# The cross-attention's weights and the gate's weights transposed by VectorE in 32x32 blocks by way of DRAM, in place of TensorE

## The chip, the core and the metric

The kernel runs on one core of a Trainium2 chip. The metric is the time of one execution on the device, in microseconds (us), as the median of several runs. The core's engines run side by side, each through its own fixed list of instructions: TensorE (PE in the rows; PEld is its loading of weights), VectorE (DVE), ScalarE (ACT), GpSimd (POOL) and SyncE (SP), which here only issues DMA transfers. They meet at semaphores. TensorE reads SBUF and writes PSUM.

## What is computed

`x` holds 64 sequences of 128 tokens of 128 channels in float32, and `ctx` 64 contexts of 77 tokens. Two stages follow each other, both with a residual:

```python
x = x + tanh(g_xattn[0]) * cross_attention(ctx, layernorm(x), Wk, Wq, Wv)
x = x + tanh(g_ffn[0])   * moe_attention(layernorm(x), sim, gates, q, k, v, o)

# moe_attention, per token, 16 experts
logits = xn @ sn - sigmoid(gates)              # xn, sn of unit length
w = softmax of relu(logits) over active experts (top 2 where none is active)
q, k, v = sum over e of w[n, e] * (x[n] @ proj[e])     # three projections
o = softmax(q k^T / sqrt(128)) v
out = sum over e of w[n, e] * (o[n] @ o_proj[e])
```

The weights of the cross-attention's softmax (128 queries by 77 keys for a sequence) are needed with the keys on the partitions, and the gate's weights `w` (tokens on the partitions, 16 experts by 4 sequences on the free axis) are needed as rows, a row of 512 tokens for an expert. Both are transposes.

## The kernel before, in words

The 64 sequences are worked in 16 groups of four (`G = 4`, 512 tokens, one PSUM bank of 512 columns). The program is written out in full by a Python loop: a head, then passes `i` of 16 steps `s`, one step for each expert. Every engine has its own `body(i)`, in which the order is written by hand: what stands at step `s` runs after the step's expert work.

In pass `i`, TensorE runs the 9 products of expert `s` for group `i` (`experts`, L1176: three projections, each as high and low halves in float16: `zq` high with `w_hi`, `zq` high with `w_lo`, `zq` low with `w_hi`), and every second step a pair of chunks of the output projection of group `i-1` or `i-2` (`y_pair`, L1188, six products). Among these lie the small products of the other groups: in pass `i` the cross-attention of group `g1 = i + 2`, and the second layer norm and the gate of group `g2 = i + 1`, and the expert attention of `gc = i - 1`.

The operand of the experts is made in a chain of three engines: VectorE multiplies `x2T_p` by a broadcast row of the gate's weights into `zq_full` (`zq_scale`, L957, four steps ahead of TensorE, `LEAD = 4`), ScalarE rounds it to the high half (`zq_high`, L612), GpSimd subtracts to get the low half (`zq_low`, L538).

The gate's path of group `g2`: the logits' products on TensorE lie among the experts of step 4 (L1231). VectorE reads them (`gate_logits` at step 4, L903 to L909), makes the mask (`gate_mask`, step 5) and the weights `w_new` (`gate_softmax`, step 6, L946). TensorE transposes `w_new` at step 8 (`w_transpose`, L1282), ScalarE copies it from PSUM to `wT` (`wT_out`, L681), SyncE writes it to the DRAM tensor `w_rows` (L405), and reads it back, two experts at a time, spread over all partitions (`spread`, `wq_bc<-w_rows`, L412, 512 KB in SBUF each, eight a group).

The cross-attention's path of group `g1`: scores at step 9 (L1239), VectorE's maximum (`x_max`, L1013), ScalarE's exponentials at step 10 (`x_exps`, L688, four), TensorE's transposes at step 12 (`px_transpose`, L1296, four of 128x77), ScalarE's copy to `pxT` (`pxT_out`, L706), and at step 14 the product with the values (`att_product`, L1303). Then VectorE adds it to `x_all` (L1024) and takes the statistics of the second layer norm.

Also at step 12 ScalarE runs `y_scale(gc, 2)` behind `pxT_out`: 8 scaled copies of the third pair's banks (L625), which TensorE's fourth pair at step 14 waits for, as it writes the same banks. At step 7 TensorE makes the output of the expert attention (`oT_p<-pcT,v_sb`, L1379), ScalarE rounds it (L791), VectorE takes the low half (`oT_low`, L972), and the first pair at step 8 waits for that.

Three other transposes already go another way: VectorE transposes 32x32 blocks (`blocks_transposed`, L892), SyncE writes the blocks to the DRAM tensor `blk_rows` (L394) and reads them back in an order in which each partition gets its row (L400, four DMAs), and a copy by ScalarE puts them in place (for instance `xn_mix` to `xnT`, L661). They serve `xn`, the expert attention's weights `pc` and its values `v`.

## Time and profile before

| | us |
|---|---|
| median of 3 runs | 841.78 |
| lowest, highest | 841.29, 841.80 |
| the profiled execution, its own time | 841.99 |
| its span, from the first to the last instruction | 839.9 |
| busy: TensorE / VectorE / GpSimd / ScalarE | 796.5 / 583.7 / 481.0 / 434.2 |
| mean granted clock of TensorE | 0.997 of full speed |

2.1 us of the profiled execution lie outside its span. All durations below come from this one execution. TensorE's products overlap in its pipeline: a product of 512 columns is shown with 0.38 us, but the next one starts 0.216 us later; what a product costs is read from the starts of its neighbours. In a timeline a row is one instruction or several of a kind in a row, with the first start and the whole length; in square brackets stands the idle time ahead and who ended it. The chain of waits goes back from the last instruction to what released each one. DMA issues stand under SPq.

### The profile page before, as it was taken

The numbers are of one execution on the slowest core, as the hardware profiler recorded it, in microseconds if no ns is written. First come the engines' busy times: TensorE is split into PE (matmuls) and PEld (weight loads), VectorE is DVE, ScalarE is ACT, GpSimd is POOL, SyncE is SP. The second block draws the span as 40 slices with busy tenths as digits, with TensorE's granted clock in tenths as the row PEclk, the third lists the DMA queues.
The fourth block names the chain that finished last, engine by engine and source line by source line (L and its number), as shares of the span: only waits on it lengthen the run. The fifth ranks groups of instructions, "written<-read, shape, count | busy, mean of one in ns | idle before, by whom it ended". The sixth has DMA issues, their size and how long they took to land.

```text
span 839.9 us, 13842 instructions
## 1 busy us (share of the span) xinstructions
PE 796.5 (95%) x4111; PEld 431.5 (51%) x4111; DVE 583.7 (69%) x1993; ACT 434.2 (52%) x1134; POOL 481.0 (57%) x702
## 2 busy tenths in 40 slices
PE   5579999999999999999999999999999999999995
PEld 4345555555555555555555555555555555544442
DVE  3767676768587676758767675876767586676647
ACT  4555646455454645545464554546455454543433
POOL 3265656564665656466665646666564665655524
PEclk9999999999999999999999999999999999999998
DMA  6373453534444333444333434443244443325100
GB/s 188 98 240 120 153 183 115 154 132 131 140 145 128 112 117 131 122 140 151 126 121 95 143 121 140 151 124 129 72 149 131 140 150 117 113 59 184 65 9 25
DMA packets 71099, 106.40 MB, mean 127 GB/s; under 512 B 6960, under 2 KB 45552, under 8 KB 71024
## 3 DMA queue, kind: packets, MB, share of 16 engines
q1 hardware_dynamic: 70304, 105.44, 40.1%
q8 instruction: 32, 0.52, 0.2%
q14 instruction: 43, 0.35, 0.1%
q10 hardware_dynamic: 720, 0.08, 0.1%
HBM read 89.51 MB, written 15.99 MB: 126 GB/s over the span
## 4 chain that ended last, share of the span: by engine, by line
PE 74%; DVE 14%; DMA 4%; issue 3%; ACT 3%; POOL 1%; SPq 1%; DVEq 0%; ACTq 0%; POOLq 0%
PE acc_q L1176 16%; PE acc_k L1176 16%; PE acc_v L1176 16%; PE y L1188 7%; PE oT_p L1188 7%; DVE x_all L986 4%; DVE zq_full L957 2%; PE oT_p L1379 2%; DVE logit L906 2%; PE m L1248 2%; PE m L1303 1%; PE m L1289 1%; ACT y_sc L625 1%; PE m L1239 1%; DMA stage<-in_L_ffn_k_proj_dram 1%
## 5 line engine op out<-in xcount | busy, mean ns | idle before, releaser
L538 POOL TENSOR_TENSOR zq<-zq_full,zq 128x512 f16<-128x512 f32 x256 | 294.9, 1161 | 298.7 <-ACT zq L612 297.5
L612 ACT ACTIVATE zq<-zq_full 128x512 f16<-128x512 f32 x256 | 160.8, 640 | 246.2 <-DVE zq_full L957 243.7
L1176 PE MATMUL acc_q<-zq,w_hi 128*128 128x512 f16 x512 | 194.6, 380 | 2.8 <-POOL zq L538 2.8
L1176 PE MATMUL acc_k<-zq,w_hi 128*128 128x512 f16 x512 | 194.5, 380 | 0.0
L1176 PE MATMUL acc_v<-zq,w_hi 128*128 128x512 f16 x512 | 194.5, 380 | 0.0
L986 DVE SCALAR_TENSOR_TENSOR x_all<-y,w_out,x_all 128x128 f32<-128x128 f32 x356 | 121.8, 342 | 80.1 <-issue 71.2
L957 DVE TENSOR_TENSOR zq_full<-wq_bc,x2T_p 128x512 f32<-128x512 f32 x256 | 167.4, 672 | 3.3 <-DMA wq_bc<-w_rows 2.5
L986 DVE SCALAR_TENSOR_TENSOR x_all<-oT_p,w_out,x_all 128x128 f32<-128x128 f32 x356 | 121.3, 341 | 0.0
L552 POOL TENSOR_TENSOR x_all<-y_sc,x_all 128x128 f32<-128x128 f32 x240 | 100.3, 454 | 20.1 <-DVE x_all L986 13.3
L1176 PE MATMUL acc_q<-zq,w_lo 128*128 128x512 f16 x256 | 97.3, 380 | 0.0
L1176 PE MATMUL acc_v<-zq,w_lo 128*128 128x512 f16 x256 | 97.3, 380 | 0.0
L1176 PE MATMUL acc_k<-zq,w_lo 128*128 128x512 f16 x256 | 97.2, 380 | 0.0
L1188 PE MATMUL y<-w_hi,oT 128*128 128x512 f16 x236 | 89.4, 379 | 4.1 <-issue 4.1
L1188 PE MATMUL oT_p<-w_hi,oT 128*128 128x512 f16 x236 | 89.4, 379 | 0.0
L1176 PEld LDWEIGHTS acc_v<-zq,w_hi 128*128 128x128 f16 x512 | 53.9, 105 | 53.9 <-issue 0.6
L1176 PEld LDWEIGHTS acc_q<-zq,w_hi 128*128 128x128 f16 x512 | 52.1, 102 | 54.0 <-issue 3.4
L1024 DVE SCALAR_TENSOR_TENSOR x_all<-m,rsum_x,x_all 128x128 f32<-128x128 f32 x64 | 18.0, 344 | 87.2 <-PE m L1303 87.2
L1176 PEld LDWEIGHTS acc_k<-zq,w_hi 128*128 128x128 f16 x512 | 50.1, 98 | 53.9 <-issue 0.6
L1188 PE MATMUL oT_p<-w_lo,oT 128*128 128x512 f16 x118 | 44.7, 379 | 0.0
L1188 PE MATMUL y<-w_lo,oT 128*128 128x512 f16 x118 | 44.6, 378 | 0.0
L625 ACT ACTIVATE y_sc<-oT_p,w_out 128x128 f32<-128x128 f32 x116 | 33.0, 369 | 19.9 <-PE oT_p L1188 19.9
L1176 PEld LDWEIGHTS acc_k<-zq,w_lo 128*128 128x128 f16 x256 | 27.0, 105 | 26.9 <-issue 0.3
(191 smaller groups left out, 1110.0 us busy)
## 6 DMA issues: line engine op xcount, KB each, us to landing
wq_bc<-w_rows SPq DMA_DIRECT2D x128, 512.0 KB, 4.4
out_dram<-x_all SPq DMA_DIRECT2D x16, 256.0 KB, 6.8
blk_rows<-v_blk SPq DMA_DIRECT2D x15, 256.0 KB, 4.2
v_mix<-blk_rows SPq DMA_DIRECT2D x60, 64.0 KB, 2.0
blk_rows<-pc_blk SPq DMA_DIRECT2D x15, 256.0 KB, 3.3
pcT<-blk_rows SPq DMA_DIRECT2D x60, 64.0 KB, 2.0
blk_rows<-xn_blk SPq DMA_DIRECT2D x13, 256.0 KB, 2.6
xn_mix<-blk_rows SPq DMA_DIRECT2D x52, 64.0 KB, 3.4
```

Of the source, the lines that this page charges most:

```text
L538: nc.gpsimd.tensor_tensor(zq[:, 1, e % Z_SLOTS, :], zq_full[:, e % F_SLOTS, :], zq[:, 0, e % Z_SLOTS, :], ALU.subtract).then_inc(zq_lo_poo ...
L552: nc.gpsimd.tensor_tensor(total, y_sc[:, n % 2, b, j, :], total, ALU.add).then_inc(y_pool_added, 1)
L612: nc.scalar.activation(zq[:, 0, e % Z_SLOTS, :], zq_full[:, e % F_SLOTS, :], ACT.Copy).then_inc(zq_hi_done, 1)
L625: last = nc.scalar.activation(y_sc[:, n % 2, b, j, :], bank[:, tok(j)], ACT.Copy, scale=w_out[:, g % 2, e, b0 + b:b0 + b + 1])
L906: link(nc.vector.tensor_tensor(logit[:], logit[:], sig[:].unsqueeze(1).broadcast_to([P, G, E]), ALU.subtract), 1)
L957: nc.vector.tensor_tensor(zq_full[:, e % F_SLOTS, :], wq_bc[:, e // 2 % W_SLOTS, e % 2], x2T_p[:], ALU.mult).then_inc(zq_full_done, 1)
L986: nc.vector.scalar_tensor_tensor(out=rows(x_all, g, b0 + b), in0=bank[:, tok(j)], scalar=w_out[:, g % 2, e, b0 + b:b0 + b + 1], in1=rows(x ...
L1024: last = nc.vector.scalar_tensor_tensor(out=rows(x_all, g, b), in0=m1[:, tok(b)], scalar=rsum_x[:, b:b + 1], in1=rows(x_all, g, b), op0=AL ...
L1176: last = nc.tensor.matmul(acc[m][:], w[:, m, s, :], zq[:, half, s % Z_SLOTS, :], start=(s == 0 and n == 0), stop=(s == E - 1 and n == 2))
L1188: last = nc.tensor.matmul(bank[:], oT[:, g % 2, half, tok(b)], w[:, O, QUAD * k:QUAD * (k + 1), :].rearrange("p e c -> p (e c)"), start=(n ...
L1248: done = nc.tensor.matmul(m1[:, tok(b)], qT[:, tok(b)], kT[:, tok(b)], start=True, stop=True)
L1379: last = nc.tensor.matmul(oT_p[:, tok(b)], v_sb[:, b, :], pcT[:, :, b, :], start=True, stop=True)
```

## The change

`w_transpose` and `wT_out` are gone. Behind `w_new` VectorE now transposes it in 32x32 blocks to `w_blk` (one instruction, 128x64, at step 6), and SyncE writes it to `w_rows` with four DMAs in place of one. `w_new` loses its zero half.

`px_transpose` stays for groups 0 and 1 alone (`P_HEAD = 2`). For the other 14 groups VectorE transposes `px` in blocks at step 11 (one instruction, 128x384; `px` is padded from 77 to 96 keys, zeroed once by GpSimd in place of `w_new`), SyncE writes `px_blk` to the DRAM tensor `px_rows`, waits for it, and reads it back with three DMAs (32, 32 and 13 keys) at step 12, and `pxT_out` copies from `px_mix` in SBUF.

```diff
+P_HEAD = 2
+S_PAD = 96
@@ SyncE
             def weight_rows(g):
-                wait(sp, wT_sb, g + 1)
-                sp.dma_start(w_rows[bass.ds(g, 1)].rearrange("a r n -> (a r) n"), wT[:]).then_inc(w_rows_in, 16)
-                wait(sp, w_rows_in, 16 * g + 16)
+                wait(sp, w_blk_done, g + 1)
+                for i in range(4):
+                    sp.dma_start(w_rows[g, :, 32 * i:32 * (i + 1)].rearrange("(k c) t -> c k t", k=2),
+                                 w_blk[32 * i:32 * (i + 1)]).then_inc(w_rows_in, 16)
+                wait(sp, w_rows_in, 64 * (g + 1))
...
+                    if s == 12 and has(g1):
+                        n = g1 - P_HEAD
+                        wait(sp, px_blk_done, n + 1)
+                        wait(sp, px_mix_in, 48 * n)
+                        sp.dma_start(px_rows.rearrange("i t r -> (i t) r"),
+                                     px_blk[:].rearrange("p j b n -> p (j b n)")).then_inc(px_blk_out, 16)
+                        wait(sp, px_blk_out, 16 * (n + 1))
+                        wait(sp, pxT_sb, g1)
+                        for j in range(3):
+                            keys = min(32, S - 32 * j)
+                            sp.dma_start(px_mix[32 * j:32 * j + keys].rearrange("t i b n -> t i (b n)"),
+                                         px_rows[:, 0:keys, P * j:P * (j + 1)].rearrange("i t r -> t i r")
+                                         ).then_inc(px_mix_in, 16)
@@ GpSimd
-            nc.gpsimd.memset(w_new[:], 0.0)
+            nc.gpsimd.memset(px[:], 0.0).then_inc(pool_set, 1)
@@ ScalarE
-            def wT_out(g):
-                wait(act, wT_ps, g + 1)
-                wait(act, w_rows_in, 16 * g)
-                nc.scalar.activation(wT[:], m0[0:E * G, 0:P], ACT.Copy).then_inc(wT_sb, 1)
...
             def pxT_out(g):
-                wait(act, pxT_ps, g + 1)
                 wait(act, att_ps, g)
-                nc.scalar.activation(pxT[:], m1[0:S, :], ACT.Copy).then_inc(pxT_sb, 1)
+                if g < P_HEAD:
+                    wait(act, pxT_ps, g + 1)
+                    nc.scalar.activation(pxT[:], m1[0:S, :], ACT.Copy).then_inc(pxT_sb, 1)
+                else:
+                    wait(act, px_mix_in, 48 * (g - P_HEAD + 1))
+                    nc.scalar.activation(pxT[:].rearrange("p (b i n) -> p b i n", b=G, n=32),
+                                         px_mix[:].rearrange("p i b n -> p b i n"), ACT.Copy).then_inc(pxT_sb, 1)
@@ VectorE, end of gate_softmax (step 6)
+                wait(dve, w_ready, g + 1)
+                wait(dve, w_rows_in, 64 * g)
+                nc.vector.transpose(w_blk[:], w_new[:, g % G_SLOTS].rearrange("p (k c) b -> p k (c b)", k=2)
+                                    ).then_inc(w_blk_done, 1)
@@ VectorE, body
+                    if s == 11 and has(g1):
+                        wait(dve, xexp_done, g1 + 1)
+                        wait(dve, px_blk_out, 16 * (g1 - P_HEAD))
+                        blocks_transposed(px_blk, px[:], px_blk_done)
@@ TensorE
-                    if s == 8 and has(g2):
-                        w_transpose(g2)
-                    if s == 12 and has(g1):
-                        px_transpose(g1)
```

How the instructions stand now is shown at three places of a pass in the middle of the program. First SyncE from step 7 to step 0 of the next pass, before:

```order
L391 DMA ctx_g<-in_ctx_dram 77x4x128 [waits ctxT_ps]
L405 DMA w_rows<-wT 64x128 [waits wT_sb]
L412 DMA wq_bc<-w_rows 128x1024 [waits zq_full_done,w_rows_in]
L412 DMA wq_bc<-w_rows 128x1024 [waits zq_full_done] x2
L422 DMA out_dram<-x_all 128x4x128 [waits y_pool_added,y_added]
L412 DMA wq_bc<-w_rows 128x1024 [waits zq_full_done] x4
```

The same stretch of SyncE now:

```order
L398 DMA ctx_g<-in_ctx_dram 77x4x128 [waits ctxT_ps]
L414 DMA w_rows<-w_blk 32x2x32 [waits w_blk_done]
L414 DMA w_rows<-w_blk 32x2x32 x3
L422 DMA wq_bc<-w_rows 128x1024 [waits zq_full_done,w_rows_in]
L422 DMA wq_bc<-w_rows 128x1024 [waits zq_full_done] x2
L432 DMA out_dram<-x_all 128x4x128 [waits y_pool_added,y_added]
L422 DMA wq_bc<-w_rows 128x1024 [waits zq_full_done]
L495 DMA px_rows<-px_blk 128x384 [waits px_mix_in,px_blk_done]
L501 DMA px_mix<-px_rows 32x4x128 [waits pxT_sb,px_blk_out]
L501 DMA px_mix<-px_rows 32x4x128
L501 DMA px_mix<-px_rows 13x4x128
L422 DMA wq_bc<-w_rows 128x1024 [waits zq_full_done] x3
```

The write of the gate's weights became four, and the four DMAs of `px` came in between the fourth and the fifth spread of the gate's weights.

Second, VectorE at steps 6 to 8, before, from the gate's last steps to the low half of `oT`:

```order
L944 RECIPROCAL wsum<-wsum 128x4 [waits gate_step]
L946 TENSOR_TENSOR w_new<-mask,wsum 128x4x16 [waits w_out_done,gate_step]
L957 TENSOR_TENSOR zq_full<-wq_bc,x2T_p 128x512 [waits zq_lo_pool]
L963 TENSOR_SCALAR rs_d<-rsum_c,out_scale 128x4 [waits rsum_c_done,scales_done]
L967 TENSOR_TENSOR w_out<-w_new,rs_d 128x64 [waits y_scaled,y_added,w_out_done]
```

VectorE at the same place now:

```order
L967 RECIPROCAL wsum<-wsum 128x4 [waits gate_step]
L969 TENSOR_TENSOR w_new<-mask,wsum 128x4x16 [waits w_out_done,gate_step]
L974 STREAM_TRANSPOSE w_blk<-w_new 128x64 [waits w_rows_in,w_ready]
L984 TENSOR_TENSOR zq_full<-wq_bc,x2T_p 128x512 [waits zq_lo_pool]
L990 TENSOR_SCALAR rs_d<-rsum_c,out_scale 128x4 [waits rsum_c_done,scales_done]
L994 TENSOR_TENSOR w_out<-w_new,rs_d 128x64 [waits y_scaled,y_added,w_out_done]
```

One transpose came in behind `w_new`, ahead of the `zq_full` of step 7. (The transpose of `px` stands likewise at step 11, between a `zq_full` and the additions of the second pair.)

Third, ScalarE from step 10 to step 14 now:

```order
L709 ACTIVATE px,sum_x<-m,nmax_x 128x77 [waits rsum_x_done,px_blk_done,xmax_done]
L709 ACTIVATE px,sum_x<-m,nmax_x 128x77 x3
L717 ACTIVATE vx<-m 77x512 [waits att_ps,vx_ps]
L635 ACTIVATE zq<-zq_full 128x512 [waits zq_used,zq_full_done]
L722 ACTIVATE x2T_p<-x2T 128x512 [waits zq_full_done,x2T_sb]
L731 ACTIVATE pxT<-px_mix 77x512 [waits px_mix_in,att_ps]
L648 ACTIVATE y_sc<-oT_p,w_out 128x128 [waits y_pool_added,y_ps,w_out_done]
```

The order is that of before, but the copy to `pxT` waits for the last of three DMAs where it waited for TensorE, and `y_scale` stands behind it.

## Rows read from the trace of the kernel before

**Rows 1.** The page, part 1: busy time and share of each engine

```profile
PE 796.5 (95%) x4111; PEld 431.5 (51%) x4111; DVE 583.7 (69%) x1993; ACT 434.2 (52%) x1134; POOL 481.0 (57%) x702
```

**Rows 2.** Chain of waits, pass 7, steps 8 and 12: start, length, what

```profile
406.30 0.11 PE m L1282
406.41 0.37 issue
406.78 0.81 PE y L1188 x3
...
418.89 0.44 PE m L1296 x4
```

**Rows 3.** Chain of waits over the whole span: TensorE's `scores`, once a pass

```profile
287.54 0.89 PE m L1248 x8
...
335.72 0.89 PE m L1248 x8
...
384.77 0.89 PE m L1248 x8
```

**Rows 4.** Timeline of TensorE, pass 7, step 14: start, length, instruction

```profile
424.34 1.06 PE L1303 MATMUL m<-vx,pxT 77*128 77x128 f32 x8
425.23 0.38 PE L1188 MATMUL y<-w_hi,oT 128*128 128x512 f16 x1
```

**Rows 5.** Timelines of VectorE and GpSimd, pass 7, steps 3 to 8

```profile
391.59 0.68 DVE L892 STREAM_TRANSPOSE pc_blk<-pc 128x512 f32<-128x512 f32 x1
...
393.91 1.19 DVE L906 TENSOR_TENSOR logit<-logit,sig 128x64 f32<-128x64 f32 x1
...
401.71 0.27 DVE L946 TENSOR_TENSOR w_new<-mask,wsum 128x64 f32<-128x64 f32 x1
...
405.99 0.69 DVE L972 TENSOR_TENSOR oT<-oT_p,oT 128x512 f16<-128x512 f32 x1 [2.13 <-ACT oT L791]
...
393.86 1.16 POOL L538 TENSOR_TENSOR zq<-zq_full,zq 128x512 f16<-128x512 f32 x1 [1.68 <-ACT zq L612]
```

**Rows 6.** Timelines of ScalarE and VectorE, pass 7, steps 10 to 12

```profile
413.46 0.21 ACT L688 ACTIVATION_READ_ACCUMULATOR px<-m,nmax_x 128x1 f32 x1
...
419.36 0.59 ACT L706 ACTIVATE pxT<-m 77x512 f32<-77x512 f32 x1 [0.79 <-PE m L1296]
420.98 1.14 ACT L625 ACTIVATE y_sc<-oT_p,w_out 128x128 f32<-128x128 f32 x4 [1.03 <-PE oT_p L1188]
...
415.10 0.35 DVE L986 SCALAR_TENSOR_TENSOR x_all<-y,w_out,x_all 128x128 f32<-128x128 f32 x1 [1.54 <-issue]
```

**Rows 7.** Timelines of VectorE and GpSimd, pass 5, step 4

```profile
296.68 0.22 DVE L906 TENSOR_TENSOR logit<-logit,sig 128x64 f32<-128x64 f32 x1
...
296.99 1.16 POOL L538 TENSOR_TENSOR zq<-zq_full,zq 128x512 f16<-128x512 f32 x1 [2.03 <-ACT zq L612]
```

**Rows 8.** Round trip of `pc`, pass 1: issue, end (PE); page part 6: landing

```profile
103.15 0.43 SPq L394 DMA_DIRECT2D blk_rows<-pc_blk  x1
...
110.33 1.13 PE oT_p L1379 x8
...
xn_mix<-blk_rows SPq DMA_DIRECT2D x52, 64.0 KB, 3.4
```

**Rows 9.** Writes of the gate's weights: issue in pass 7; landing of all 16

```profile
406.75 0.45 SPq L405 DMA_DIRECT2D w_rows<-wT  x1
...
DMA to landing us min/median/max: 1.7/2.2/3.8
```

**Rows 10.** Timelines of ScalarE and TensorE, pass 0, steps 10 and 14

```profile
79.13 0.21 ACT L688 ACTIVATION_READ_ACCUMULATOR px<-m,nmax_x 128x1 f32 x1
...
87.42 1.06 PE L1303 MATMUL m<-vx,pxT 77*128 77x128 f32 x8
```

**Rows 11.** Head: timeline of VectorE, then the chain of waits

```profile
36.21 0.27 DVE L946 TENSOR_TENSOR w_new<-mask,wsum 128x64 f32<-128x64 f32 x1
...
38.95 3.27 DMA w_rows<-wT
```

More of the change, by code:

```diff
@@ L966, in out_weights @@
                 wait(dve, y_scaled, 4 * (g - 1))
[L967 removed]
+                nc.vector.tensor_tensor(w_out[:, g % 2], w_new[:, g % G_SLOTS],
                                         rs_d[:].unsqueeze(1).broadcast_to([P, E, G]), ALU.mult).then_inc(w_out_done, 1)
@@ L1276, in kx_product @@
                 nc.tensor.matmul(m1[:, 0:G * S], m_kq[:], ctxT[:], start=True, stop=True).then_inc(kxT_ps, 1)
-            def w_transpose(g):
-                wait(pe, w_ready, g + 1)
-                if g == X_HEAD - 2:
-                    wait(pe, xnT_sb, X_HEAD)
-                nc.tensor.transpose(m0[:, 0:P], w_new[:, g % G_SLOTS].rearrange("p h e b -> p (h e b)"),
-                                    ident[:]).then_inc(wT_ps, 1)
             def vx_product(g):
-                wait(pe, wT_sb, cap(g))
+                wait(pe, logit_read, cap(g))
                 wait(pe, xnT_sb, g + 1)
@@ L1295, in px_transpose @@
                 for b in range(G):
-                    last = nc.tensor.transpose(m1[0:S, tok(b)], px[:, b, :], ident[:])
+                    last = nc.tensor.transpose(m1[0:S, tok(b)], px[:, b, 0:S], ident[:])
                 last.then_inc(pxT_ps, 1)
```

31 lines of the change are left out of this document (17 added, 14 removed).

## The prediction, made before the changed kernel ran

> **What bounds the kernel now.** The first view is the page's busy table: TensorE is busy for 95% of the span, the next engine for 69% [rows 1]. So what the change takes from TensorE counts, if nothing else is late where it is taken. Whether it is shows in the second view, the chain of waits. Over the whole span it passes TensorE's `scores` once a pass: from pass to pass 49.05 us (335.72 to 384.77), and 48.18 us in one pass (287.54 to 335.72) [rows 3]. The distance is the same from pass 2 to pass 13 but for that one, so pass 7, around 400 us, stands for them. In it the chain leaves TensorE once: between the logits of step 4 and the first output pair of step 8 it runs over VectorE (L906, the additions, the mask, a `zq_full`) and ScalarE, and TensorE waits for what comes out. From step 8 to the next step 4 it stays on TensorE. That split decides the two halves of the change, since one of the removed transposes lies in each part.
>
> **Gate transpose on TensorE: worth nothing in most passes.** The transpose takes 0.11 us of TensorE at 406.30, and behind it TensorE stands still for 0.37 us until the output pair starts at 406.78 [rows 2]. That start is set by VectorE: the low half of `oT` starts at 405.99, takes 0.69 us, ends at 406.68 [rows 5], and the pair follows 0.1 us later. Nothing in the chain to that instruction passes through the removed transpose or ScalarE's copy of it, which stands behind ScalarE's work on `oT`. So without it TensorE waits 0.48 us in place of 0.37, and the pair starts when it did. Gain 0. Only in pass 1, where the pair is not yet waiting for VectorE, is 0.11 us gained.
>
> **Transposes of the cross-attention's weights: 0.44 us each.** At step 12 four of them take 0.44 us, in the stretch in which the chain never leaves TensorE [rows 2]. 14 of 16 groups lose them, in passes 0 to 13. Full worth would be 14 x 0.44 = 6.2 us. It is full worth only where the new way round is ready for step 14.
>
> **The new way round, in a pass of the middle.** The last exponential ends at 413.67 (413.46 + 0.21) [rows 6]. VectorE is idle then, for 1.54 us until 415.10, where it waits for the second output pair [rows 6], so its new transpose costs its neighbours nothing. The same instruction on 512 columns takes 0.68 us [rows 5]; for 384 I take 0.56, and it ends at 414.28. Then come a DMA out, a wait, three DMAs in. The nearest row is the round trip of `pc` in pass 1, the one place where TensorE waited for such a trip: issued at 103.15, with TensorE released at 110.33, that is 7.2 us with four DMAs in and 256 KB [rows 8]. Here they are three and 192 KB: less one issue of 0.43 us, and a little for the size, 6.6 us. The data are in at 420.9, and ScalarE's copy (0.65 us with its start, as the copy from PSUM now takes 0.59 [rows 6]) ends at 421.6. Who waits? First the product of step 14, which stood at 424.34 [rows 4] and would like to start 0.44 us earlier, at 423.9: 2.3 us to spare. Second, and tighter, the 8 scaled copies queued behind it on ScalarE: the first four take 1.14 us from 420.98 [rows 6], all eight about 2.2, and the fourth output pair, at 425.23 [rows 4] and then 424.79, waits for them. Counting back, with 0.07 us for the release, the copy to `pxT` may end at 422.5; it ends at 421.6. So 0.9 us to spare, and the trip may take up to 7.5 us before a pass loses anything, 8.0 until the gain is gone.
>
> **What else moves.** VectorE's transpose of `w_new` (128x64, 0.25 us with its wait, as its neighbours of that size, `w_new` itself 0.27 [rows 5]) lies ahead of an idle time of 2.13 us that ends with L972 [rows 5], so it is hidden; if that cover were gone it would cost 0.25 us a pass. SyncE issued the write of the weights at 406.75 [rows 9]; `w_new` is done at 401.98 [rows 5], so the four writes can go from 402.3 on, 0.45 us apart as the one of now, and even with the slowest landing of such a write in the trace (3.8 us, against 2.2 in the median [rows 9]) the spreads start earlier than now. That also clears the queue ahead of the trip of `px`. Behind SyncE's new wait at step 12 stand the fifth and sixth spreads, which VectorE needs six steps later: nothing. The scaled copies start at 421.6 in place of 420.98, so GpSimd gets its two `zq` of steps 13 and 14 about 0.6 us later and may hand the second norm on some 0.5 us late; I cost it at nothing, as ScalarE and TensorE have other work ahead of what needs it, and at 0.5 us a pass if they hadn't. ScalarE's own 16 copies of the gate's weights are gone, off the chain.
>
> **Pass 0** has no output pairs, so its steps are shorter. The exponentials end at 79.34 and the product of step 14 starts at 87.42 [rows 10], to become 86.9 without the two transposes. The new way: 79.34 + 0.6 for VectorE + 6.6 to 7.2 for the trip + 0.65 for the copy = 87.2 to 87.8. I take 87.6: 0.2 us later than now. Bounds: 0.55 us gained if the trip is hidden, 1.5 lost if it takes 1.3 us more.
>
> **The head.** `w_new` of group 0 is done at 36.48, but the write to DRAM is issued only at 38.95, behind TensorE and ScalarE, and lands 3.27 us later [rows 11], so the first spread goes at 42.2. Now the first of four writes goes at 36.8 and the last at 38.2. If it lands in 2.2 to 3.8 us [rows 9] the spread starts at 40.4 to 42.0, 0.2 to 1.8 us earlier. I take 1.1.
>
> Here the Trainium skill speaks against the change. The row shows one write landing in 3.27 us [rows 11]. The page "DMA: Bandwidth & Descriptors", Specifications, says that pieces under 512 bytes are below line rate, as the engine then reads, modifies and writes; the four writes of the gate's weights go in pieces of 128 bytes, which no row here has on this path. By that rule they land late, and the head's gain would fall to its lower end, with the sum 0.9 us higher. In the passes it would change nothing, as there are over 2 us to spare.
>
> **The sum.** Passes 2 to 13: 12 x 0.44 = 5.3 us gained. Pass 1: 0.44 + 0.11 = 0.55. Pass 0: 0.2 lost. Head: 1.1. Together 6.7 us. Against the profiled execution's 841.99 us that is 835.3, and as that lies 0.2 above the median of 841.78, the median becomes 835.1. By the bounds of pass 0 and the head alone: 833.5 to 837.5. I add 1 us above for small waits that I don't see: 833 to 838.5.
>
> **Rivals.** First, **a turn-over between VectorE and GpSimd**. L906, an operation of 0.22 us, takes 1.19 us at 393.91, and ends when GpSimd's L538, started at 393.86, 0.05 us before it, ends [rows 5]. In pass 5 L906 came first (296.68 against 296.99), took 0.22 us [rows 7], and that pass is the one of 48.18 us: 0.87 us shorter [rows 3]. So two instructions race with a margin of 0.05 us, and the winner is worth 0.87 us a pass. If the change shifts GpSimd's or ScalarE's queue by more than that up to step 4, 12 further passes gain: 12 x 0.87 = 10.4 us, and 824.7. For it: ScalarE and GpSimd are shifted by some 0.5 us at steps 13 to 0. Against it: both have idle time ahead of the race (GpSimd waits 1.68 us for ScalarE [rows 5]), and both racers start from the same output pair of step 2. 18%. The page "SBUF — State Buffer", Who interferes with whom, has the rule: an operation with two inputs in SBUF and one of GpSimd that reads SBUF exclude each other, and issue order decides; by that rule, the trace agrees with 1.19 against 0.22 us.
>
> Second, **slower: the round trip of `px` comes late.** Place: ScalarE's copy to `pxT` at step 12 with the scaled copies behind it. It decides from 8.0 us on, and costs 1 us a pass for each us beyond. For it: the trips in the loop share the queue with 512 KB spreads, and the reads back of `xn` land in 3.4 us in the median [rows 8]: with that, and the last of three issues 0.86 us behind the first, a way out of 3.7 us already gives 8.0, just the point. With 8.6 us, 13 passes lose 0.6 each: 13 x 0.6 = 7.8, less 1.1 of the head, so 848.5 (841.78 + 6.7). Against it: the spreads are earlier now. 14%.
>
> Third, **no gain**: trip and queue take 7.5 to 8.0 us, or GpSimd's lateness reaches TensorE's transposes of step 2, and the 0.44 us are waited away in each pass. Then the head's gain is what stays: 841.78 - 1.1 = 840.7, within 838.5 to 842. 16%.
>
> **How the numbers follow.** Forecast 52%: 835.1, in its own range 833 to 838.5. Turn-over 18%: 824.7. No gain 16%. Slower 14%: from 843.5 on. The range takes in forecast, turn-over and most of the third case, and leaves out the slower one and a little: 824.5 to 841. About 0.2% (1.7 us) is what a measurement of this kernel can tell from no change: faster means under 840.1. Forecast, turn-over and half the third give 0.78; same 0.10; slower 0.12.
>
> **What would show it.** In the trace after: the distance of `scores` from pass to pass falls from 49.05 to 48.6; the wait of the first output pair behind step 8's experts grows to about 0.5 us; TensorE has no wait at step 14; ScalarE's copy to `pxT` ends 3 us ahead of it, with the trip of `px` at 6.6 us; L906 stays at 1.19 us; the first spread is issued at about 41; TensorE is busy for less by the transposes. Wrong would be: a distance near 47.7 with L906 at 0.22 (the first rival); idle time of TensorE at step 14 ahead of an output pair, released by ScalarE's `y_sc` (the second); a distance of 49 with new waits at step 2 (the third).

## The result, and the profile after

Before and after, six runs each: 841.65 us (840.91 to 842.15) against **833.17 us** (831.46 to 837.11); ratio 0.9907, 95% interval 0.9881 to 0.9932. The change makes the kernel about 8.5 us faster. The forecast was 835.1 us in a range of 824.5 to 841.0. Note the spread: 1.2 us for the kernel before, 5.6 us for the changed one. The execution profiled is the slowest of the six, 837.11 us with a span of 835.3, and 4.9 us under the profiled one of before (841.99). So its rows have to explain both why it is faster and why others are faster still.

The page of the changed kernel, part 1: busy time of each engine.

```profile
PE 790.2 (95%) x4039; PEld 423.4 (51%) x4039; DVE 593.7 (71%) x2023; ACT 430.0 (51%) x1118; POOL 481.2 (58%) x702
```

TensorE has 72 instructions and 6.3 us less than in [rows 1], VectorE 30 and 10 us more.

The chain of waits at the `scores` of passes 5 to 8, and the first output pair of step 8 of pass 2 from the timeline of TensorE (start, length, instruction, idle ahead of it):

```profile
288.78 0.89 PE m L1279 x8
...
337.67 0.89 PE m L1279 x8
...
386.30 0.89 PE m L1279 x8
...
434.21 0.89 PE m L1279 x8
```

```profile
164.91 0.38 PE L1219 MATMUL y<-w_hi,oT 128*128 128x512 f16 x1 [0.48 <-issue]
```

The distance from pass to pass, 49.05 us in [rows 3], is 48.63 us in most passes (pass 7, 386.30 to 434.21, and three others, explained below, have 47.7 to 47.9; pass 5, 288.78 to 337.67, has 48.89). The wait ahead of the pair is 0.48 us, 0.11 more than in [rows 2]. From the `scores` of pass 2 (142.88) to those of pass 14 (768.98) the kernel gains 7.1 us. But pass 2 itself starts 2.5 us **later** than before (142.88 against 140.39). So the passes gained more than forecast, and the beginning, where 1.45 us were to be won, lost.

Two rows show the first half of that loss. Timeline of TensorE in pass 0, step 2, and its windows (us, busy and instructions, granted clock, DMA share, GB/s), changed kernel:

```profile
56.88 1.11 PE L1286 MATMUL m<-ident,x 128*128 128x128 f32 x4 [2.99 <-ACT x L656]
```

```profile
56.00:60.00 4.00, 3.12 (x10) 0.50 0.64 193
60.00:64.00 4.00, 4.00 (x18) 0.66 0.64 198
```

The experts' products of pass 0 start 2.5 us earlier than before, but the second norm that pass 0 needs next is only 1.4 us earlier, so TensorE stands still for 2.99 us (1.04 before). Behind that the granted clock is 0.50, the lower of its two levels (1.2 GHz), and products of 512 columns come 0.43 us apart, where they come 0.216 us apart at 1.00.

The clock of the first products needs care. The profile's record of the granted clock begins only at 40 to 55 us (49.1 in this execution, 53.2 in the one before), and ahead of its first entry a window prints 1.00 whatever the clock was; the mean of 0.997 given for the kernel before leaves that stretch out too. The spacing of the products fills the gap. In all 14 traces of this document the first products of pass 0 come 0.43 us apart. Two neighbours in the kernel before:

```profile
50.55 0.63 PE L1176 MATMUL acc_k<-zq,w_hi 128*128 128x512 f16 x1
50.98 0.63 PE L1176 MATMUL acc_k<-zq,w_lo 128*128 128x512 f16 x1
```

How long that lasts differs from execution to execution: to 48.9 us in this one, to 53.1 in the one before, to 50.6 in the run with the gate's half alone (1, below). That early change here is the rest of the 2.99 us: with the same head, but a clock that rose later, TensorE stood still for 1.80 us there.

The second half of the loss is the new trip in pass 0, here from SyncE, ScalarE and TensorE (write out, reads back, copy, product of step 14):

```profile
80.70 0.32 SPq L495 DMA_DIRECT2D px_rows<-px_blk  x1
85.89 1.25 SPq L501 DMA_DIRECT2D px_mix<-px_rows  x3
88.64 0.63 ACT L731 ACTIVATE pxT<-px_mix 77x512 f32<-77x512 f32 x1 [4.41 <-DMA px_mix<-px_rows]
...
89.32 0.94 PE L1327 MATMUL m<-vx,pxT 77*128 77x128 f32 x6 [1.46 <-ACT pxT L731]
```

"Trip" means, from here on, from the issue of that write (80.70) to the start of ScalarE's copy (88.64): 7.94 us here and 8.74 us in pass 1, where the fourth output pair waits 0.88 us for `y_sc`. In pass 2 it is 6.47 us, and nobody waits:

```profile
172.44 0.98 SPq L495 DMA_DIRECT2D px_rows<-px_blk  x1
176.17 1.24 SPq L501 DMA_DIRECT2D px_mix<-px_rows  x3
178.91 0.63 ACT L731 ACTIVATE pxT<-px_mix 77x512 f32<-77x512 f32 x1 [2.20 <-DMA px_mix<-px_rows]
...
182.03 1.06 PE L1327 MATMUL m<-vx,pxT 77*128 77x128 f32 x8
```

Two more numbers for later: `px_blk` takes 0.578 us each and `w_blk` 0.245 us; the four small writes of the gate's weights land in 1.3/1.5/3.9 us (minimum, median, maximum), the single write of before in 1.7/2.2/3.8 [rows 9].

**Where the extra gain in the passes comes from.** VectorE's subtraction of the sigmoid (L929, L906 before) against GpSimd's `zq` (L561), in a usual pass of the changed kernel (3) and in pass 7:

```profile
200.60 1.16 POOL L561 TENSOR_TENSOR zq<-zq_full,zq 128x512 f16<-128x512 f32 x1 [1.68 <-ACT zq L635]
200.65 1.19 DVE L929 TENSOR_TENSOR logit<-logit,sig 128x64 f32<-128x64 f32 x1
```

```profile
395.43 0.22 DVE L929 TENSOR_TENSOR logit<-logit,sig 128x64 f32<-128x64 f32 x1
395.88 1.16 POOL L561 TENSOR_TENSOR zq<-zq_full,zq 128x512 f16<-128x512 f32 x1 [1.56 <-ACT zq L635]
```

This is the race of [rows 5] and [rows 7]. "Turned over" means that VectorE comes first and its subtraction is short. Among passes 2 to 13 of the profiled execution of before that was so in one pass; in this one in four (subtractions at 395.43, 589.25, 636.99 and 684.86). Three more passes at 0.72 to 0.9 us each, less 0.26 us lost in pass 5, are what the passes gained beyond 12 x 0.42.

### The profile page after: what moved, and what is told of

Its sections match the earlier page's. It is cut to its first block, busy times and chain, and to the rows that moved or that the text cites. A ratio compares the mean times of both kernels' runs of the same rounds, so it can differ in the third digit from the quotient of the medians.

```text
span 835.3 us, 13855 instructions
## 1 busy us (share of the span) xinstructions
PE 790.2 (95%) x4039; PEld 423.4 (51%) x4039; DVE 593.7 (71%) x2023; ACT 430.0 (51%) x1118; POOL 481.2 (58%) x702
## 4 chain that ended last, share of the span: by engine, by line
PE 73%; DVE 12%; DMA 5%; ACT 4%; issue 3%; SPq 2%; POOL 1%; DVEq 0%; ACTq 0%; POOLq 0%
PE acc_q L1207 16%; PE acc_k L1207 16%; PE acc_v L1207 15%; PE y L1219 8%; PE oT_p L1219 7%; DVE x_all L1013 4%; DVE zq_full L984 2%; DMA px_rows<-px_blk 2%; PE oT_p L1402 2%; ACT y_sc L648 2%; PE m L1279 2%; PE m L1327 2%; DVE logit L929 1%; PE m L1270 1%; PE m L1313 1%
## 5 line engine op out<-in xcount | busy, mean ns | idle before, releaser
L561 POOL TENSOR_TENSOR zq<-zq_full,zq 128x512 f16<-128x512 f32 x256 | 295.9, 1165 | 294.0 <-ACT zq L635 293.8
L1219 PEld LDWEIGHTS y<-w_hi,oT 128*128 128x128 f16 x236 | 22.9, 97 | 31.2 <-ACT oT L816 7.6
```

The costliest lines, as they stand in the source:

```text
L561: nc.gpsimd.tensor_tensor(zq[:, 1, e % Z_SLOTS, :], zq_full[:, e % F_SLOTS, :], zq[:, 0, e % Z_SLOTS, :], ALU.subtract).then_inc(zq_lo_poo ...
L1219: last = nc.tensor.matmul(bank[:], oT[:, g % 2, half, tok(b)], w[:, O, QUAD * k:QUAD * (k + 1), :].rearrange("p e c -> p (e c)"), start=(n ...
```

## Experiments

Theory going in: the passes gain by the cross-attention's transposes alone (0.44 us each); the gate's is worth nothing there; the beginning loses by the fallen clock and by two long trips; the race is a separate cost of 0.87 us a pass. Rivals: the gate's transpose counts too; the fall of the clock is not tied to the idle time; the subtraction is long for another reason. "Scores of pass 2" is the start of TensorE's `scores` there in the timeline: 140.23 before, 142.72 in the changed kernel.

### 1 and 2: one half of the change alone

Gate alone (cross-attention's weights transposed by TensorE in every pass; SyncE's and VectorE's steps for them run only from `P_HEAD` on, and so never):

```diff
-P_HEAD = 2
+P_HEAD = 99
+                    if s == 12 and has(g1):
+                        px_transpose(g1)
```

Cross-attention alone (gate part as before):

```diff
-                nc.vector.transpose(w_blk[:], ...).then_inc(w_blk_done, 1)
+                    if s == 8 and has(g2):
+                        w_transpose(g2)
...
-                for i in range(4):
-                    sp.dma_start(w_rows[g, :, 32 * i:32 * (i + 1)]...)
+                sp.dma_start(w_rows[bass.ds(g, 1)].rearrange("a r n -> (a r) n"), wT[:]).then_inc(w_rows_in, 16)
```

> Only the gate's weights are transposed by VectorE by way of DRAM; the cross-attention's weights stay with TensorE in every pass. Theory (the gate transpose is worth nothing in a pass, since TensorE then waits for VectorE before the first output pair of step 8; it brings only an earlier first expert product): distances of the scores stay 49.05 us, that wait is 0.48 instead of 0.37 us, and the time is 839 to 842 against 841.7, the upper end if the early start is given back to a fallen clock in pass 0. Rival (its removal counts in every pass, 0.11 x 12): another 1.3 us less and distances of 48.94.

> Only the cross-attention's weights go over VectorE and DRAM; the gate's stay with TensorE and ScalarE. Theory: all of the gain in the passes comes from here: distances of 48.6 us, so 12 x 0.44 = 5.3 us less than before from pass 2 on, less up to 1.5 us lost in passes 0 and 1 by the long trips there: 836 to 837.5. No 2.99 us idle of TensorE and no fallen clock at 56 to 62 us. If the gate part were worth something in a pass, this would be worse than the changed kernel by more than 1 us.

**Gate alone: 840.2 us** (839.46 to 841.18, 11 runs), ratio 0.9983 (0.9974 to 0.9992). Every distance from pass 2 to pass 13 is 49.05 to 49.07 us, the wait ahead of the pair at step 8 is 0.48 us:

```profile
209.36 0.38 PE L1219 MATMUL y<-w_hi,oT 128*128 128x512 f16 x1 [0.48 <-issue]
```

So in this surrounding the gate's transpose is worth nothing in a pass, as the theory has it. What it gains, 1.6 us, it gains at the beginning: scores of pass 2 at 138.11, 2.1 us earlier than before. Its head is that of the changed kernel, but the wait ahead of the second norm is 1.80 us and not 2.99, and no fall of the clock follows at 56 to 62 us. (Its record shows 0.50 at 44 to 51 us. That is the slow stretch of the first products; the other records, but for kernel 4's, begin too late to show it.)

**Cross-attention alone: 833.2 us** (831.54 to 835.37, 4 runs), ratio 0.989 (0.9876 to 0.9904): as fast as the whole change, and faster than expected (836 to 837.5). No clock fell at 56 to 62 us; the first products were slow until 54.5. What the traced execution shows of the difference is again the race, turned over in four of the twelve passes from 2 to 13. At 835.37 us it is the slowest of the four executions; that the faster ones have more such passes was seen in no trace.

### 3: TensorE kept busy in pass 0

```diff
+                    if s == 2 and i == 0:
+                        for r in range(12):
+                            nc.tensor.matmul(y0[:], w_hi[:, K, 2, :],
+                                             w_hi[:, Q, 0:4, :].rearrange("p e c -> p (e c)"), start=True, stop=True)
                     if s == 2 and has(g2):
                         x2_transpose(g2)
```

> The changed kernel, with 12 products (2.6 us) that nobody reads put into TensorE's idle 2.99 us ahead of the second-norm transposes of pass 0. Theory (the granted clock fell to 0.50 at 56 to 62 us because TensorE had been idle there, at a cost of about 2.3 us): the clock stays near 1.00 there, the products are 0.216 us apart, and the time is 2 to 2.5 us less than the changed kernel's in executions in which its clock falls. Rival (the fall has another cause, or comes in one execution and not in another): clock still 0.50 there, or a time equal to the changed kernel's fastest (831.5).

The same windows of TensorE in this kernel:

```profile
56.00:60.00 4.00, 4.00 (x22) 1.00 0.68 178
60.00:64.00 4.00, 4.00 (x26) 1.00 0.72 215
```

The clock stays up, `scores` of pass 1 start at 93.94 instead of 96.15: 2.2 us, the expected amount. But this doesn't show that the 12 products did it. In this execution the first products were slow until 52.2 us and not only until 48.9, so TensorE came to this place at 55.3, and the second norm's data were ready at 56.8, as in the changed kernel: without the 12 products it would have waited some 1.5 us, not 2.99. What speaks for the idle time as the cause is the comparison of traces. Of the eleven without such products, two have a fall at 56 us, and they are the two with the longest wait at this place (2.99 us, and 2.88 in kernel 8); the other nine have at most 1.86 us and no fall there. Kernels 7 and 8 wait once more in pass 0, for 2.92 and 2.48 us, and there too a fall follows.

And yet the **time is 835.31 us** (832.25 to 836.47, 6 runs), no better than the changed kernel's 833.17. The expectation of the time failed. The profiled execution (835.47 us) shows one reason: of the twelve passes from 2 to 13 only two were turned over. The 2.2 us at the beginning are of the size of two and a half turned-over passes, and the number of those differs from execution to execution; so does the clock of the first products. As long as the race runs, a time of this kernel can't answer a question of 2 us. So the race had to go first.

### 4 and 5: the race taken away, in both kernels

An operand in PSUM instead of SBUF for the subtraction (4 is the changed kernel with it, 5 the kernel before with it):

```diff
-                nc.vector.tensor_tensor(logit[:], lg, rnorm2[:]...broadcast_to([P, G, E]), ALU.mult)
+                lg2 = m0[:, G * E:2 * G * E].rearrange("p (b e) -> p b e", e=E)
+                nc.vector.tensor_tensor(lg2, lg, rnorm2[:]...broadcast_to([P, G, E]), ALU.mult)
...
-                nc.vector.tensor_tensor(logit[:], logit[:], sig[:]..., ALU.subtract)
+                nc.vector.tensor_tensor(logit[:], lg2, sig[:]..., ALU.subtract)
```

> The changed kernel, in which the scaled gate logits are kept in PSUM between the two steps, so that the subtraction of the sigmoid reads one operand from SBUF and one from PSUM. Theory (the 1.19 us subtraction of 0.22 us stands behind GpSimd's subtraction because both of its operands are in SBUF; it is worth 0.87 us a pass): the subtraction takes about 0.2 us in all passes, distances of 47.75 instead of 48.6 in the 8 passes that had it long, so 7 to 8 us less: 824 to 826. Rival (one SBUF operand is enough to be held up, or TensorE then waits for something else next): 1.19 us and no change, or a gain of less than 3 us.

> The kernel before, with only the scaled gate logits kept in PSUM, as in the run that took the changed kernel to 825.5. Theory (the collision with GpSimd is a cost of its own, 0.87 us a pass, that does not depend on who transposes): the subtraction is short in every pass, distances of 48.18 instead of 49.05 in the passes 2 to 12 that had it long, so 10 to 11 us less than before: 831 to 832. The change would then be worth 5 to 6.5 us between the two kernels without the collision. Rival (the change frees the queue of VectorE so that the collision matters only with it): less than 5 us less than before.

**4: 825.53 us** (824.8 to 827.94, 5 runs), ratio 0.9814 (0.9801 to 0.9826), and **5: 830.84 us** (830.63 to 831.35, 4 runs), ratio 0.9872 (0.9858 to 0.9887). Both as the theory expected. VectorE and GpSimd in the changed kernel with the edit:

```profile
194.66 1.16 POOL L562 TENSOR_TENSOR zq<-zq_full,zq 128x512 f16<-128x512 f32 x1 [1.68 <-ACT zq L636]
194.72 0.22 DVE L936 TENSOR_TENSOR logit<-m,sig 128x64 f32<-128x64 f32 x1
```

The order is the losing one, GpSimd first by 0.06 us, and the subtraction takes 0.22 us all the same: it is short in all 16 groups of both kernels. So it was held up only while both of its operands lay in SBUF. The distances are 47.77 us (changed) and 48.22 (before): the difference of 0.45 us is the four transposes, and 10.6 us of the kernel before (841.46 us, measured beside 5) had been this one wait. Without the race the change is worth 830.84 - 825.53 = 5.3 us.

### 6: the halves again, without the race

The kernel with cross-attention alone, and the edit of 4:

> The cross-attention's weights by VectorE and DRAM, the gate's weights by TensorE and ScalarE, logits kept in PSUM. It differs from the 825.5 us kernel in the gate's transpose alone. Theory (the gate's transpose hid in TensorE's wait for VectorE at step 8; without the collision that wait is gone, so the transpose now counts): distances of 47.88 instead of 47.77, which is 1.3 us over 12 passes, and with the later start of the head 827.5 to 829. Rival (the gate part is worth nothing anywhere): 825.5 within 0.7.

**6: 831.19 us** (830.13 to 832.63, 4 runs), ratio 0.9872 (0.9854 to 0.989). That is 5.7 us more than the whole change, where 2 to 3.5 were expected, and as much as the kernel before with the same edit: here the cross-attention's half alone is worth **nothing**. Its trips are 7.9 to 8.5 us long, those of the 825.5 us kernel 6.5 to 7.9, six of eleven under 7.0 (passes 2 to 12). SyncE's timeline in a pass of each, cross-attention alone first:

```profile
210.39 0.49 SPq L415 DMA_DIRECT2D w_rows<-wT  x1
212.21 1.29 SPq L422 DMA_DIRECT2D wq_bc<-w_rows  x3
213.66 0.39 SPq L432 DMA_DIRECT2D out_dram<-x_all  x1
216.89 0.32 SPq L422 DMA_DIRECT2D wq_bc<-w_rows  x1
217.62 0.32 SPq L495 DMA_DIRECT2D px_rows<-px_blk  x1
222.79 1.24 SPq L501 DMA_DIRECT2D px_mix<-px_rows  x3
```

```profile
202.26 1.71 SPq L415 DMA_DIRECT2D w_rows<-w_blk  x4
205.03 2.55 SPq L423 DMA_DIRECT2D wq_bc<-w_rows  x3
210.32 0.39 SPq L433 DMA_DIRECT2D out_dram<-x_all  x1
213.54 0.32 SPq L423 DMA_DIRECT2D wq_bc<-w_rows  x1
214.27 0.32 SPq L496 DMA_DIRECT2D px_rows<-px_blk  x1
218.08 1.24 SPq L502 DMA_DIRECT2D px_mix<-px_rows  x3
```

The write of the blocks goes out 28.87 us after the pass's `scores` in both (188.75 and 185.41). But the three spreads of 512 KB start 5.4 us ahead of it in the first and 9.2 us in the second. Windows just ahead of that write and over it (us, granted clock, DMA share, GB/s), first kernel, then second:

```profile
216.00:217.00 1.00, 1.00 1.06 254
217.00:218.00 1.00, 1.00 0.95 372
218.00:219.00 1.00, 1.00 1.09 369
```

```profile
212.00:213.00 1.00, 1.00 0.18 51
213.00:214.00 1.00, 1.00 0.00 0
214.00:215.00 1.00, 1.00 0.43 152
```

In the first the write enters DMA engines that are full, in the second empty ones. The expectation had the wrong mechanism (the 0.11 us of TensorE). The new theory: the gate's half is worth most of the 5.7 us because its earlier writes clear the DMA engines ahead of the other half's trip.

### 7, 8 and 9: the trip made longer, its traffic moved

A second write in the trip (7); the gate's writes and spreads held back (8), both in the 825.5 us kernel; and the store of the output (`out_dram<-x_all`) moved behind the trip in the 831.2 us kernel (9):

```diff
+                        sp.dma_start(px_more.rearrange("i t r -> (i t) r"),
+                                     px_blk[:].rearrange("p j b n -> p (j b n)")).then_inc(px_more_out, 16)
+                        wait(sp, px_more_out, 16 * (n + 1))
                         wait(sp, pxT_sb, g1)
                         for j in range(3):
```

```diff
                     if s == 9 and has(g2):
+                        wait(sp, zq_full_done, E * i + 9 + LEAD + 1)
                         weight_rows(g2)
```

```diff
-                    if s == 11 and has(gd):
-                        store(gd)
...
+                    if s == 13 and has(gd):
+                        store(gd)
                     if s == 14:
                         spread_q(g2, 4)
```

> The 825.5 us kernel, in which SyncE writes the transposed blocks of the cross-attention's weights a second time, to another place, and waits for that too before it reads them back: the trip grows by one write's landing, 2.3 to 3.9 us, from 6.6 us to 9 to 10.5. Theory (a trip of up to 7.5 us is hidden, each microsecond beyond it is lost in every pass): 1.5 to 3 us lost in each of 12 passes, distances of 49.3 to 50.8, 843 to 861. Rival (the output pairs are not what ends the trip's slack, and it is much longer): under 3 us lost in all.

> The 825.5 us kernel, in which SyncE holds the writes of the gate's weights, and with them the three spreads behind them, back until VectorE has done its product of step 9: some 5 us later, 0.2 us later than where the 831.2 us kernel (gate's weights by TensorE) writes them. Nothing else differs. Theory (the gate part is worth 5.7 us there because its earlier writes let three spreads of 512 KB each and the store of the output drain ahead of the other trip, which falls from 8.1 to 6.6 us, under the 7.75 us from which it costs): trips of 8.0 to 8.4 us, distances of 48.0 to 48.4, 829 to 831. Rival (the 0.11 us transpose or ScalarE's copy is what costs): 825.5 within 1, trips of 6.6.

> The 831.2 us kernel (cross-attention's weights by VectorE, the gate's by TensorE, logits kept in PSUM), in which SyncE issues the store of the output (256 KB) behind the blocks' trip and not 4 us ahead of it. Theory (the blocks' write is held up by what is still on its way in the DMA engines, which are 0.9 to 1.09 busy from 1.5 us after the three spreads to 2.4 us after the write; the store is about a seventh of these bytes): the trip falls from 8.1 to 7.3 to 7.6 us, under the 7.86 us from which it costs there, distances of 47.9 instead of 48.2: 827.5 to 829. Rival (the three spreads alone fill that time, or the wait has nothing to do with the queue): trips of 7.9 to 8.4 and 830.5 to 832.

**7: 844.55 us** (842.24 to 850.13, 11 runs), ratio 1.0041 (1.0024 to 1.0059). The second write landed in under 2 us, so the trips grew to 8.2 to 9.6 us and not to 10.5, and most distances stayed under the 49.3 us expected. The rival, under 3 us lost in all, is out: 19 us were lost. A pass with 9.2 us:

```profile
365.80 0.32 SPq L498 DMA_DIRECT2D px_rows<-px_blk  x1
370.50 0.32 SPq L501 DMA_DIRECT2D px_more<-px_blk  x1
372.36 1.24 SPq L507 DMA_DIRECT2D px_mix<-px_rows  x3
375.02 0.63 ACT L737 ACTIVATE pxT<-px_mix 77x512 f32<-77x512 f32 x1 [4.95 <-DMA px_mix<-px_rows]
...
377.74 0.39 PE L1231 MATMUL y<-w_hi,oT 128*128 128x512 f16 x1 [0.88 <-ACT y_sc L654]
```

TensorE waits for `y_sc`, as the forecast's second rival described.

**8: 850.53 us** (849.09 to 854.43, 4 runs), ratio 1.0103 (1.0087 to 1.0118). The direction is the theory's, the size is not: 829 to 831 was expected. With the hold the write of `w_rows` goes out 0.2 us later than in the 831.2 us kernel, as intended, but the spreads 1.2 us later, since four writes take 1.7 us to issue where one takes 0.5. The blocks' write then lands in 6.7 us in the median (5.5 in the 831.2 us kernel, 4.0 in the 825.5 us one), the trips are 8.3 to 9.8 us.

**9: 826.42 us** (825.96 to 828.11, 5 runs), ratio 0.9825 (0.9811 to 0.9838): 4.8 us less than the 831.2 us kernel, 1 us better than expected. All trips from pass 2 on are 6.7 to 7.8 us and all distances 47.77 or 47.78, with the gate's transpose still on TensorE. So that transpose costs nothing in a pass here either: the output pair of step 8 starts 21.34 us after `scores` in kernels 4 and 9, behind a wait of 0.14 us in 4 and 0.03 in 9. The traces split the 5.7 us. Passes 2 to 13 take 578.9 us in kernel 6, 573.9 in 4 and 573.3 in 9: what the passes lost, 5 us, was the trip's. The beginning is apart from that: scores of pass 2 at 140.35 us in 6, 137.63 in 4 and 140.80 in 9. There kernel 9 gets nothing back; its median is 0.9 us above that of 4.

The trips and distances of these kernels and of 4, 6, 11 and 12, 77 passes (2 to 12) of seven kernels, lie on one line. Some of them, read from the timelines:

```
trip us         6.47   7.54   7.77   7.86   8.06   8.39   8.93   9.22   9.60
distance us    47.77  47.77  47.78  47.87  48.08  48.40  48.94  49.23  49.62
kernel             4      9      9      6      6      6      7      7      7
```

distance = 47.77 + (trip - 7.76) where the trip is above 7.76 us, and 47.77 below, within 0.03 us but for 14 passes. Eleven of these are off by 0.04 to 0.3 us; in ten of the eleven the blocks' write already goes out 0.1 to 0.3 us later after `scores` than the usual 28.87, so that time was lost ahead of the trip. Three, of kernels 7 and 8, are 1.7 us longer, 51.3 to 51.5 us; there the granted clock fell to 0.50 for 3.4 us behind TensorE's waits for ScalarE, as in pass 12 of kernel 7 (window, busy, clock, DMA share, GB/s). Other passes with the same waits kept the clock.

```profile
670.00:680.00 10.00, 8.79 (x36) 0.83 0.23 82
```

The line says what a trip costs; it doesn't say what makes a trip long. Between kernels that is the traffic, as 8 and 9 show. But in the changed kernel and in kernel 4, eleven trips of 7.2 to 8.0 us (passes 5 to 7 and 10 to 12) stand beside eleven of 6.4 to 6.9 us with nearly the same issue times. Ahead of each of the long ones the three spreads had landed at least 1.6 us and the store at least 0.8 us before the blocks' write went out. Their cause is open.

### 10, 11 and 12: the beginning

10 is the kernel of 3 with `P_HEAD = 4`, so that TensorE transposes the cross-attention's weights in passes 0 and 1 too; 11 the same in the 825.5 us kernel; 12 the 825.5 us kernel with the products of 3.

```diff
-P_HEAD = 2
+P_HEAD = 4
+                    if s == 12 and g1 < P_HEAD:
+                        px_transpose(g1)
```

> The changed kernel with the 12 idle products of pass 0, and with TensorE's transposes of the cross-attention's weights kept in passes 0 and 1 too. Theory (the long trips of 7.9 and 8.7 us cost 1.5 and 0.9 us of TensorE's waiting there against 0.44 us of transposes each): the waits ahead of the product of step 14 in pass 0 and of the fourth output pair in pass 1 go, and the scores of pass 2 start 1.2 to 1.5 us earlier than in the run with the 12 products alone (at 138.5 instead of 139.95); 833.5 to 835 against its 835.3, as many passes as there turned over. Rival (the lost time of pass 0 is taken up by another wait): scores of pass 2 at 139.95 or later.

> The 825.5 us kernel, with TensorE's transposes of the cross-attention's weights kept in passes 0 and 1. Theory: the trips of these passes cost only 0.3 and 0.46 us of waiting in this kernel, as much as the two transposes of 0.44 us: 825 to 826, no change. Rival (the longer trips delay more than TensorE's two waits show): 824.3 or less.

> The 825.5 us kernel with 12 products that nobody reads in TensorE's idle time ahead of the second-norm transposes of pass 0 (1.86 to 2.99 us there). Theory (the kernel's executions differ by whether and where the granted clock falls to half, and a fall at 56 to 62 us comes from that idle time): the executions from 826.4 to 827.9 go, all lie at 824.5 to 826, clock 1.00 from 50 us on; where the clock falls ahead of the first expert product instead, the 12 products cost up to 0.8 us. Rival (the spread has nothing to do with it): median and spread stay as they are, 825.5 with 3 us between the ends.

**10: 835.26 us** (835.07 to 836.08, 5 runs), ratio 0.9928 (0.9915 to 0.9942). Scores of pass 2 at 138.25 instead of 139.95, 1.7 us earlier (1.2 to 1.5 expected). Yet the time is that of kernel 3, above the 833.5 to 835 expected, and the spread is 1.0 us instead of 4.2: with all trips at 6.2 to 6.6 us every distance is 48.63, and the race is turned over in no pass from 2 to 13. **11: 825.68 us** (824.76 to 828.32, 5 runs), ratio 0.9822 (0.9807 to 0.9836): no change, as expected. **12: 825.10 us** (824.32 to 825.86, 5 runs), ratio 0.9803 (0.979 to 0.9816): the median fell by 0.4 us, which the intervals don't separate, and the slow end went from 827.94 to 825.86, as expected, though with five runs each. That the clock did it isn't shown. The traced execution of kernel 4 has no fall at 56 to 62 us to begin with, and in kernels 4 and 11 the fastest executions have the lower mean clocks on record (0.993 at 824.80, 824.99 and 824.76 us), which in the traced one is the early slow stretch, as its record begins at 40 us. 12 has the lowest median of all versions, within the noise of 4 and 11.

**What turns the race over.** Kernels 3 and 10, cross-attention alone and the changed kernel together have 44 trips in passes 2 to 12. Nine of them take 7.21 to 7.76 us, and the subtraction of the next pass is short after all nine. The other 35 take up to 6.83 or from 7.83 us on, and it is long after all 35. (Outside these passes the upper bound doesn't hold: it is short behind 8.18 us in pass 1 of kernel 3 and behind 7.92 us in pass 13 of cross-attention alone.) The changed kernel's GpSimd, behind a trip of 6.47 us and one of 7.62 us, 9.18 and 8.02 us ahead of the `scores` of the timeline (191.35, 386.13):

```profile
182.17 1.16 POOL L561 TENSOR_TENSOR zq<-zq_full,zq 128x512 f16<-128x512 f32 x1 [4.23 <-ACT zq L635]
```

```profile
378.11 2.27 POOL L561 TENSOR_TENSOR zq<-zq_full,zq 128x512 f16<-128x512 f32 x2 [5.39 <-ACT zq L635]
```

The longer trip makes ScalarE's copy and its scaled copies 1.16 us later, and so GpSimd's queue. GpSimd is then still 1.14 us late with the norm after `scores`, and its `zq` of the race starts at 9.75 us after `scores` instead of 9.25, while VectorE's subtraction starts at 9.30 in both. The kernels without the held-up subtraction (4 and later) agree up to here: in the 11 passes behind kernel 9's trips GpSimd comes 0.05 us ahead up to a trip of 7.06 us, and behind 7.33 to 7.77 us it comes 0.14 to 0.56 us after VectorE, growing with the trip. Why the old order is back above 7.76 us stays open. One would think that TensorE is late by what the trip exceeds that, and that VectorE's side moves with it; but in kernel 6, behind trips of 7.86 to 8.48 us, VectorE comes first by 0.55 us in 8 of 11 passes.

## Why the prediction was right, point by point

- **Gate transpose worth nothing in the passes: right**, shown twice (49.05 to 49.07 us with the gate's half alone; 47.77 in kernel 9). The wait of 0.48 us is to the hundredth what was forecast.
- **0.44 us a pass for the cross-attention's transposes: right.** 0.42 in the changed kernel, 0.45 without the race. `px_blk` took 0.578 us (0.56 taken), `w_blk` 0.245 (0.25).
- **Trip 6.6 us: right for the undisturbed pass** (6.4 to 6.7 in five of the eleven passes from 2 to 12), but not a constant: the others had 7.2 to 8.0. What was missing is that its length depends on the spreads and the store still under way (kernels 6, 8 and 9), and on something more that stays open, since ahead of the changed kernel's own long trips of passes 5 to 7 and 10 to 12 the three spreads and the store had landed. The forecast said of the earlier spreads "That also clears the queue ahead of the trip of `px`" and gave that no value; without the race it is worth some 5 us.
- **It may take 7.5 us, break-even 8.0: nearly right.** Measured 7.76 and, with 0.45 above it, 8.2. The chain that sets it, ScalarE's scaled copies and the fourth output pair, is the one of the forecast. From pass 2 on, passes 5 and 7 of the changed kernel exceeded it (8.01 and 7.92 us, 0.26 and some 0.16 lost).
- **Pass 0 and pass 1: wrong.** The step that failed is the trip "6.6 to 7.2" taken for pass 0, and for pass 1 the assumption that it behaves as a middle one: 7.94 and 8.74 us. In pass 0 the bound of "1.5 lost if it takes 1.3 us more" was nearly used up (TensorE waited 1.46 us, of which 0.44 is the gain given back). In kernel 10 the two passes are 1.7 us better without the new way; a gain of 0.24 by it had been forecast.
- **Head: the write earlier, right; the gain, not in this execution.** The first spread went at 39.8 instead of 42.2, better than the 41 forecast and outside its 40.4 to 42.0, since the small writes landed fast, in 1.5 us in the median against 2.2 for the single write. By the Trainium skill, page "DMA: Bandwidth & Descriptors", Specifications, transfers under 512 bytes are below line rate; a cost of that in the landing of 8 KB in pieces of 128 bytes is not what these rows show. The gain itself came where the clock stayed up: the gate's half alone is 1.6 us faster, 1.1 was forecast. The term that failed in the profiled execution is what the gain would meet: TensorE started earlier, its clock rose earlier, it ran into an idle time of 2.99 us, and the clock fell. The `scores` of pass 1 came 2.2 us later than in kernel 3. How often this happens stays open.
- **The sum** of 6.7 us came to 4.9 in the profiled execution: about 4 us too much at the beginning (1.45 gained forecast, 2.5 lost), about 2 too little in the passes (5.3 forecast, 7.1 gained). The passes' extra is the first rival's, so the total is close in part by luck: two errors of opposite sign.
- **First rival, the turn-over (18%): it came in part**, in four passes (one of them in exchange for the one of before) and not in twelve. The argument against it, that ScalarE and GpSimd have idle time ahead of the race, failed: it took up only a part of a shift of 1.16 us, and 0.5 us of it reached the race. The price of 0.87 us, and the rule of the Trainium skill that a VectorE instruction with two inputs in SBUF and a GpSimd instruction that reads SBUF contend (page "SBUF — State Buffer", Who interferes with whom), both hold: with one of the operands in PSUM the operation took 0.22 us in the same place.
- **The median** of 833.17 us is 1.9 us under the forecast's. Its profiled execution is the slowest of six. That the faster ones have more passes turned over, or no fallen clock, fits the small spread of kernel 10, in which nothing was turned over, but was seen in no trace of them. How often each happens stays open.

## What to carry to other kernels

A wait that two engines race for is a cost even in a kernel that looks bound by a third: look for an instruction whose length in the timeline is five times its usual one, and remove it before measuring anything of its size. When a transfer is put on a path with a known slack, ask what is in the DMA engines at the moment of its issue, and not only how long it takes in the median: moving a store that nobody waits for was worth 4.8 us here. An earlier start of the bottleneck engine is a gain only as far as its next input is earlier too. And before a fall of the clock is given as a cause, look where its record begins, and read the spacing of the products ahead of that.

## What the hardware showed beyond the forecast

- VectorE's subtraction of two SBUF operands (128x64) takes 0.22 us alone and 1.19 us when GpSimd's operation of 1.16 us started 0.05 us before it; with one operand in PSUM it takes 0.22 us beside the same operation.
- TensorE's first products of pass 0 came 0.43 us apart in all 14 traces, the spacing of the lower level (1.2 GHz), until 48.9 us in one execution and 55.3 in another. In pass 0 the granted clock fell to 0.50 once more behind idle times of 2.99 and 2.88 us (at 56 us, changed kernel and kernel 8) and of 2.92 and 2.48 us (at 89 and 90 us, kernels 7 and 8), and not behind those of up to 1.86 us at 56 us; and in three passes of kernels 7 and 8 behind two waits of 0.5 to 0.7 and 0.9 us, while other passes with such waits kept 1.00.
- The write of 192 KB landed in 4.0 us in the median where the DMA engines had drained (kernel 4), and in 5.5 and 6.7 us where 1.5 MB of spreads had been issued from 5.4 and 4.2 us ahead of it on, with the store behind them (6 and 8); in 4.7 us in kernel 9, with the spreads as in 6 and without the store.
